# SP fetches each plain tile ahead of the shifted tile, and GpSimd fetches the coefficients of the last four blocks

## Chip, core and metric

One core of a Trainium2 chip runs the whole program. The metric is the device time of one launch in microseconds, the median of several runs. Its engines are PE (TensorE), DVE (VectorE), ACT (ScalarE), POOL (GpSimd) and SP (SyncE, which here only issues transfers). All transfers, whichever engine issues them, run on the core's 16 DMA engines.

## What is computed

```
x = x + _L0_conv_ref(_gn(x), L0_conv_offset)
x = x + _L1_conv_ref(_gn(x))
```

`x` is 16 images of 384 channels of 32 x 32 pixels, fp32. `_gn` is a group normalisation over 12 channels and all pixels of an image. `_L0_conv_ref` takes the 384 channels as 48 blocks of 8; each block is displaced by its own whole-pixel offset (zeros come in from outside) and then convolved with its own 3 x 3 Gaussian:

```
shifted = x[:, ch[:, None, None], iyc[:, :, None], ixc[:, None, :]]
shifted = shifted * mask[None]
out = lax.conv_general_dilated(shifted, kern_c[:, None, :, :], window_strides=(1, 1), padding='SAME', feature_group_count=C, ...)
```

Only blocks whose offset is under 32 pixels on both axes have anything left inside the image. `_L1_conv_ref` multiplies the 384 channels of every pixel by a Hadamard matrix.

## The kernel before

The program has four stages.

**Load and statistics** (to about 87 us): SP loads the 16 images into a ring of 12 places in SBUF, DVE and ACT take their statistics, and the coefficients of the group normalisation go to `gn_rows` in HBM (a semaphore `gn_out` marks them as written).

**The block stage** (about 88 to 133 us), which the change touches. `FAST` = 9 blocks (k = 0 to 8) are displaced and convolved. A tile holds one block as 128 partitions (16 images x 8 channels) of 1024 pixels, 512 KB. Each block needs two tiles from HBM and one small table:

- the *shifted* tile k (`fetch_shifted`, L302 to L306), read at the displaced address into one of `DEEP` = 3 buffers; it may be issued when PE has transposed shifted tile k-3 (`flipped`);
- the *plain* tile k (`fetch_plain`, L308 to L316), the same channels undisplaced, into one of `WIDE` = 5 buffers (`own_x`: three of `blk`, `other_a`, a piece of `parts`). Tiles 3 and 4 may be issued when block k-3 is finished by DVE (`x1_done`), because their buffers hold something else before that; tiles 5 to 8 when block k-5 has had its statistics and has *landed* in HBM (`blk_out`);
- the coefficients of block k (`fetch_gn`, L288 to L291): 128 x 2 numbers, 1 KB, from `gn_rows`.

Every fetch first reads its address from SBUF into a register (a TENSOR_LOAD) and then issues its transfer. SP fetches all of these but the coefficients of block 2, in an order written out by hand: shifted 0 to 4 and plain 0 to 2 already lie in SBUF or under way before the stage begins; then come the coefficients of 0, 1, 3, 4, and then for each k from 5 the coefficients of k, shifted k, plain k-2.

Per block, ACT subtracts the mean from the shifted tile (`centre`, L472), PE transposes it in 8 pieces (L578), ACT masks the upper and DVE the lower half of it (L491, L851), PE convolves by 20 matmuls (L588), DVE adds the result to the plain tile (`partial`, L855; for blocks 0 and 1 also L887) and takes its statistics (L874, L876), and POOL writes the finished tile to `x1_rows` in HBM (`leave`, L409; ACT writes its statistics, L484). PE's order is: transposes of k+1, then the convolution of k. DVE's is: mask of k+1, `partial` of k, statistics of k. The offset and convolution weights are ready long before.

POOL's only computing work in this stage is at its start: two products of 128 x 1024 (L415), for blocks 0 and 1, then the nine `leave`.

**Between the stages** (133 to 146 us): SP waits until all block statistics are in HBM, reads them back (L370), and the second normalisation's coefficients are worked out. POOL waits until all nine blocks have landed and then gathers them into the ring (L284).

**The Hadamard stage** (146 us to the end): 16 images are normalised, multiplied and stored; DVE is busy nearly throughout.

Of the kernel before, what the change touches and what calls it, by code (L numbers as in the profile page):

```python
# [33 lines left out]
DEEP = 3  # L34
WIDE = 5
EARLY = 2
FAST = 9
# [76 lines left out]
def build(nc, x_pad, offset, geo, had, out):  # L114
# [8 lines left out]
    with ctx:  # L123
# [3 lines left out]
        def sem(name):  # L127
            return ctx.enter_context(nc.semaphore(name))
# [103 lines left out]
        gn_out = sem("gn_out")  # L232
# [18 lines left out]
        def bc(ap, shape):  # L251
            return ap.broadcast_to(shape)
# [21 lines left out]
        def fast_blocks_out(eng):  # L274
            for u in range(WIDE):
                eng.wait_ge(blk_out[u], 16 * blocks_in(u))

        def gather_part(eng, n, limit, signal):

            first, count = PARTS[n]  # L280
            at = place_of(first + BATCH) if first < EXTRA else place_of(first)
            runs = x1_rows[0:limit, :].rearrange("c (g n) -> (c g) n", n=count * PIXELS)
            for t in range(CT):
                eng.indirect_dma_start(ring[:, t, at:at + count, :].rearrange("p b n -> p (b n)"), None,  # L284
                                       runs, bass.IndirectOffsetOnAxis(ap=row_at[:, n, t:t + 1], axis=0),
                                       bounds_check=limit * BATCH // count - 1, oob_is_err=False).then_inc(signal, 16)

        def fetch_gn(eng, k):  # L288

            at = eng.value_load(place[0:1, k, 0:1], min_val=0, max_val=CHANNELS - BIND)  # L290
            eng.dma_start(blk_gn[:, k, :], gn_rows[ds(at, BIND), :].rearrange("c (b k) -> b c k", k=2)).then_inc(gn_in[k], 16)  # L291
# [3 lines left out]
        def _(sp):  # L295
# [4 lines left out]
            def fetch_shifted(k):  # L300

                at = sp.value_load(place[0:1, k, 2:3], min_val=1, max_val=PIXELS * (CHANNELS - BIND + 2) - 1)  # L302
                if k >= DEEP:
                    sp.wait_ge(flipped, k - DEEP + 1)
                sp.dma_start(blk[:, DEEP + k % DEEP, :],
                             x_pad[:, ds(at, BIND * PIXELS)].rearrange("b (c n) -> b c n", c=BIND)).then_inc(shift_in[k % DEEP], 16)  # L306

            def fetch_plain(k):  # L308
                at = sp.value_load(place[0:1, k, 1:2], min_val=PIXELS, max_val=PIXELS * (CHANNELS - BIND + 1))  # L309
                if k >= WIDE:  # L310
                    sp.wait_ge(blk_stat_done, k - WIDE + 1)
                    sp.wait_ge(blk_out[k % WIDE], 16 * (k // WIDE))
                elif k >= DEEP:
                    sp.wait_ge(x1_done, k - DEEP + 1)
                sp.dma_start(own_x[k % WIDE],
                             x_pad[:, ds(at, BIND * PIXELS)].rearrange("b (c n) -> b c n", c=BIND)).then_inc(x_in[k % WIDE], 16)  # L316
# [21 lines left out]
            for k in (0, 1, 3, 4):  # L338
                fetch_gn(sp, k)
            for k in range(DEEP + EARLY, FAST + 2):  # L340
                if k < FAST:
                    fetch_gn(sp, k)
                    fetch_shifted(k)
                fetch_plain(k - 2)


            active = sp.value_load(count_i[0:1, 0:1], min_val=0, max_val=OFFSETS)
# [56 lines left out]
        @block.gpsimd  # L404
        def _(pool):
            def leave(k, u):

                pool.wait_ge(x1_done, k + 1)
                pool.dma_start(x1_rows[BIND * k:BIND * (k + 1), :].rearrange("c (b n) -> b c n", b=BATCH), own_x[u]).then_inc(blk_out[u], 16)  # L409


            image = [128, HEIGHT, WIDTH]
            for k in range(EARLY):
                pool.wait_ge(slope_ready, k + 1)
                pool.tensor_tensor(aside[k].rearrange("p (y x) -> p y x", y=HEIGHT),  # L415
                                   bc(share[:, k, 1, :].rearrange("p (y o) -> p y o", o=1), image),
                                   bc(share[:, k, 0, :].rearrange("p (o x) -> p o x", o=1), image), ALU.mult).then_inc(mean_share, 1)
            pool.wait_ge(rank_done, 1)
            pool.wait_ge(place_done, 1)
            for k in range(FAST):  # L420
                leave(k, k % WIDE)
            active = pool.value_load(count_i[0:1, 0:1], min_val=0, max_val=OFFSETS)

            fast_blocks_out(pool)
            with pool.If(active > FAST):
                pool.wait_ge(more_out, 32 * (OFFSETS - FAST))
            pool.wait_ge(rows_ready, 1)
            with pool.If(active > FAST):
                for n in range(KEPT):
                    gather_part(pool, n, CHANNELS, more_patched)  # L430
                pool.wait_ge(more_patched, 16 * CT * KEPT)
            for n in range(KEPT):
                gather_part(pool, n, FAST * BIND, part_in[n])
            for j in range(EXTRA):
                pool.wait_ge(reload_done[j], 16)
                with pool.If(active > FAST):
                    gather_part(pool, KEPT + j, CHANNELS, more_patched)
                    pool.wait_ge(more_patched, 16 * CT * (KEPT + j + 1))
                gather_part(pool, KEPT + j, FAST * BIND, part_in[KEPT + j])
# [544 lines left out]
```

## Time and profile before

| | |
|---|---|
| median of 3 runs | 258.5 us (257.35 to 259.47) |
| the profiled execution | 258.53 us, of it 256.7 us span |
| granted TensorE clock, mean | 0.862 |
| PE, DVE, ACT, POOL busy | 55%, 77%, 53%, 16% of the span |
| DMA | 76.79 MB, mean 299 GB/s |

In a row of the timeline the start and the duration stand first, then engine, line, operation, output<-inputs, count, and in brackets how long the engine sat idle before it and what released it. "SPq" is SP's sequencer. A TensorE clock of 1.00 is the upper of two levels and 0.50 the lower. In a table of stretches "DMA share" is the busy share of the 16 DMA engines; overlapping packets can put it a little over 1.

### The profile page before, as it was taken

How to read it: one execution, taken by the hardware profiler on the slowest of the kernel's cores; microseconds unless marked ns; L12 is line 12 of the kernel's file. 1: busy time of each engine (PE TensorE's matmuls, PEld its weight loads, DVE VectorE, ACT ScalarE, POOL GpSimd, SP SyncE). 2: the span in 40 equal slices, each digit the busy share in tenths (PEclk: the TensorE clock that was granted, in tenths of full speed). 3: DMA queues.
4: the chain of work that ended last, by engine and by line, in shares of the span. 5: the costliest groups of instructions: out<-in, count | busy, mean ns of one | idle time of the engine just before them, and what ended most of it. 6: DMA issues, size and time to landing. Idle time of an engine off the chain costs nothing.

```text
span 256.7 us, 2310 instructions
## 1 busy us (share of the span) xinstructions
PE 141.8 (55%) x616; PEld 85.4 (33%) x616; DVE 197.4 (77%) x321; ACT 136.2 (53%) x217; POOL 41.4 (16%) x39
## 2 busy tenths in 40 slices
PE   0000000607406349877921696999999999989610
PEld 0000000407406339776811522343333333333200
DVE  0799999999973179855750338999999999999930
ACT  1000999779762045143301399997787777770000
POOL 0000000000000052100113782000704383000000
PEclk9999999965955559979975569999999999999975
DMA  5999999999999307999970657229999999998798
GB/s 167 419 409 410 408 410 290 373 410 409 409 295 248 84 5 211 314 335 270 261 168 14 179 187 258 92 89 372 354 321 416 360 417 409 421 417 325 278 407 343
DMA packets 26222, 76.79 MB, mean 299 GB/s; under 512 B 7968, under 2 KB 8224, under 8 KB 25920
## 3 DMA queue, kind: packets, MB, share of 16 engines
q1 hardware_dynamic: 19616, 67.12, 72.0%
q0 software_dynamic: 4752, 9.45, 12.1%
q10 hardware_dynamic: 1840, 0.06, 0.5%
q8 instruction: 5, 0.08, 0.1%
q14 instruction: 9, 0.07, 0.1%
HBM read 67.07 MB, written 29.99 MB: 378 GB/s over the span
## 4 chain that ended last, share of the span: by engine, by line
DVE 39%; DMA 32%; SPq 10%; issue 6%; ACT 5%; PE 4%; ACTq 1%; DVEq 0%
DMA ring<-x_pad 27%; DVE ring L950 22%; DVE parts L272 10%; DMA blk<-x_pad 4%; ACT blk L533 3%; PE ps L569 2%; DVE blk L272 2%; SPq L291 2%; SPq L290 2%; ACT parts L541 2%; SPq L302 1%; PE ps L588 1%; DVE blk_half L874 1%; SPq L309 1%; DVE halfstat L814 1%
## 5 line engine op out<-in xcount | busy, mean ns | idle before, releaser
L950 DVE SCALAR_TENSOR_TENSOR ring<-ps,beta,ring 128x1024 f32<-128x1024 f32 x48 | 59.7, 1276 | 0.0
L650 PE MATMUL ps<-parts,had_sb 128*128 128x512 f16 x216 | 54.1, 385 | 8.0 <-DVE parts L272 5.7
L578 PE MATMUL ps<-geo_sb,blk 128*128 128x128 f32 x72 | 13.6, 353 | 57.5 <-DMA blk<-x_pad 45.2
L284 POOL DMA_INDIRECT ring<-x_rows,row_at x24 | 32.4, 1349 | 50.1 <-DMA ring<-x_pad 37.7
L814 DVE BATCH_NORM_STATS2 halfstat<-ring 128x6 f32<-128x512 f32 x64 | 38.8, 671 | 1.7 <-DMA ring<-x_pad 1.7
L533 ACT ACTIVATE blk<-ring,gn 128x1024 f32<-128x1024 f32 x32 | 37.8, 1225 | 0.0
L272 DVE TENSOR_TENSOR parts<-blk,parts 128x1024 f16<-128x1024 f32 x27 | 32.8, 1216 | 6.0 <-ACT parts L541 4.1
L588 PE MATMUL ps<-parts 128*128 128x160 f32 (+2 forms) x180 | 30.3, 329 | 10.6 <-ACT parts L463 10.2
L650 PEld LDWEIGHTS ps<-parts,had_sb 128*128 128x128 f16 x216 | 20.1, 99 | 44.0 <-DVE parts L272 13.2
L588 PEld LDWEIGHTS ps<-parts 128*128 128x128 f32 x180 | 29.0, 210 | 11.9 <-ACT parts L463 10.6
L660 PE MATMUL ps<-ring,first_w 128*128 128x512 f32 x64 | 32.0, 624 | 0.0
L578 PEld LDWEIGHTS ps<-geo_sb,blk 128*128 128x128 f32 x72 | 11.1, 182 | 58.8 <-issue 52.7
L541 ACT ACTIVATE parts<-blk 128x1024 f16<-128x1024 f32 x27 | 27.2, 1041 | 0.1
L472 ACT ACTIVATE blk<-blk,blk_gn 128x1024 f32<-128x1024 f32 x7 | 8.0, 1148 | 22.8 <-DMA blk<-x_pad 13.1
L453 ACT ACTIVATE other_a<-ring 128x1024 f32<-128x1024 f32 x16 | 18.3, 1143 | 0.0
L455 ACT ACTIVATE parts<-ring 128x1024 f32<-128x1024 f32 x16 | 18.3, 1141 | 0.0
L415 POOL TENSOR_TENSOR other_a<-parts 128x1024 f32<-128x1024 f32 x1 | 1.9, 1903 | 91.6 <-DVE parts L880 91.6
L660 PEld LDWEIGHTS ps<-ring,first_w 128*128 128x128 f32 x64 | 12.2, 198 | 10.7 <-issue 10.2
L525 ACT ACTIVATE first_w<-geo_sb,gn 128x128 f32<-128x128 f32 x16 | 6.4, 398 | 13.6 <-PE ps L650 12.4
L445 ACT ACTIVATE parts<-parts 128x396 f32<-128x396 f32 x1 | 0.5, 532 | 23.8 <-DVE parts L749 23.8
L569 PE MATMUL ps<-moment,geo_sb 128*128 128x16 f32 (+1 forms) x28 | 6.4, 389 | 11.6 <-DVE moment L835 11.6
L855 DVE SCALAR_TENSOR_TENSOR blk<-ps,blk_gn,blk 128x1024 f32<-128x1024 f32 x6 | 7.6, 1273 | 5.1 <-DMA blk<-x_pad 5.0
(115 smaller groups left out, 133.7 us busy)
## 6 DMA issues: line engine op xcount, KB each, us to landing
ring<-x_pad SPq DMA_DIRECT2D x20, 1536.0 KB, 15.3
out<-ring SPq DMA_DIRECT2D x13, 1536.0 KB
blk<-x_pad SPq DMA_DIRECT2D x15, 512.0 KB, 17.1
out<-ring SPq DMA_DIRECT2D x9, 512.0 KB
x_rows<-blk POOLq DMA_DIRECT2D x6, 512.0 KB, 7.5
other_a<-x_pad SPq DMA_DIRECT2D x2, 512.0 KB, 8.6
x_rows<-other_a POOLq DMA_DIRECT2D x2, 512.0 KB, 6.4
geo_sb<-geo SPq DMA_DIRECT2D x1, 683.0 KB, 4.6
```

The costliest lines, as they stand in the source:

```text
L272: eng.tensor_tensor(part_of(n, t, 1), scaled(n, t), part_of(n, t, 0), ALU.subtract).then_inc(low_done[t], 1)
L284: eng.indirect_dma_start(ring[:, t, at:at + count, :].rearrange("p b n -> p (b n)"), None, runs, bass.IndirectOffsetOnAxis(ap=row_at[:, n, ...
L453: act.activation(aside[0], image, ACT.Identity, bias=image[:, 0:1], scale=-1.0, accum_out=sums[:, 0, i:i + 1])
L455: act.activation(aside[1], image, ACT.Square, bias=image[:, 0:1], scale=-1.0, accum_out=sums[:, 1, i:i + 1]).then_inc(sum_stat_done, 1)
L533: act.activation(scaled(n, t), ring[:, t, place_of(i), :], ACT.Identity, bias=gn[:, t, i % BATCH, 1:2], scale=gn[:, t, i % BATCH, 0:1]).th ...
L541: act.activation(part_of(n, t, 0), scaled(n, t), ACT.Copy).then_inc(high_done[t], 1)
L578: last = pe.transpose(pixels[:, j // 4, 128 * (j % 4):128 * (j % 4 + 1)], shifted[:, 128 * j:128 * (j + 1)], eye)
L588: last = pe.matmul(sums[:, bank, 32 * (lo - 16 * bank):32 * (hi - 16 * bank)], pixels[:, j, :], weights[:, lo - (4 * j - 1):hi - (4 * j - ...
L650: last = pe.matmul(ps[n % 4][:, h, :], had_sb[:, sign, :], part_of(n, t, part)[:, 512 * h:512 * (h + 1)], start=False, stop=ends and part ...
L660: pe.matmul(ps[n % 4][:, h, :], first_w[:, n % 2, :], ring[:, 0, place_of(n + EXTRA), 512 * h:512 * (h + 1)], start=True, stop=False, skip ...
L814: last = dve.bn_stats(halfstat[:, i % 4, t, h, :], ring[:, t, place_of(i), 512 * h:512 * (h + 1)])
L950: dve.scalar_tensor_tensor(ring[:, m, place_of(i), :], ps[n % 4][:, :, :].rearrange("p a n -> p (a n)"), beta[:, i % BATCH:i % BATCH + 1], ...
```

## The change

SP's loop from k = 5 issues plain k-2 first and then shifted k, and no longer fetches coefficients. POOL fetches the coefficients of blocks 5 to 8 after its two products and before its first `leave`.

```
             for k in (0, 1, 3, 4):
                 fetch_gn(sp, k)
             for k in range(DEEP + EARLY, FAST + 2):
+                fetch_plain(k - 2)
                 if k < FAST:
-                    fetch_gn(sp, k)
                     fetch_shifted(k)
-                fetch_plain(k - 2)
...
+            pool.wait_ge(gn_out, 16)
+            for k in range(DEEP + EARLY, FAST):
+                fetch_gn(pool, k)
             pool.wait_ge(rank_done, 1)
             pool.wait_ge(place_done, 1)
             for k in range(FAST):
                 leave(k, k % WIDE)
```

Nothing else differs; the line numbers below the first hunk move by one or two.

On SP, at the start of the loop, the kernel before has the coefficients of block 5 (L290, L291), shifted 5 (L302, L305) and plain 3 (L309, L315, whose destination is `other_a`):

```order
L290 TENSOR_LOAD place
L290 ISA x2
L291 ISA
L291 DMA blk_gn<-gn_rows 128x1x2
L302 TENSOR_LOAD place
L302 ISA x2
L305 REGISTER_ALU [waits flipped]
L305 DMA blk<-x_pad 128x1x1024
L309 TENSOR_LOAD place
L309 ISA x2
L315 REGISTER_ALU [waits x1_done]
L315 DMA other_a<-x_pad 128x1x1024
```

The changed kernel has at the same place plain 3 and then shifted 5:

```order
L309 TENSOR_LOAD place
L309 ISA x2
L315 REGISTER_ALU [waits x1_done]
L315 DMA other_a<-x_pad 128x1x1024
L302 TENSOR_LOAD place
L302 ISA x2
L305 REGISTER_ALU [waits flipped]
L305 DMA blk<-x_pad 128x1x1024
```

The wait for `x1_done` now stands ahead of shifted 5. Near the loop's end, plain 5 (which waits for block 0 to have landed, `blk_out0`), shifted 7, plain 6 and shifted 8 stand in this order in the changed kernel:

```order
L315 REGISTER_ALU [waits blk_out0,blk_stat_done]
L315 DMA blk<-x_pad 128x1x1024
L302 TENSOR_LOAD place
L302 ISA x2
L305 REGISTER_ALU [waits flipped]
L305 DMA blk<-x_pad 128x1x1024
L309 TENSOR_LOAD place
L309 ISA x2
L315 REGISTER_ALU [waits blk_out1,blk_stat_done]
L315 DMA blk<-x_pad 128x1x1024
```

Before, each shifted tile stood ahead of that wait, so that shifted 7 and 8 waited for no block to land; now each stands behind one. On POOL the kernel before goes straight from the products to `leave`:

```order
L415 TENSOR_TENSOR other_a<-parts 128x1024 [waits slope_ready]
L415 TENSOR_TENSOR parts<-parts 128x1024 [waits slope_ready]
L409 DMA x_rows<-blk 16x8x1024 [waits x1_done,place_done,rank_done]
```

In the changed kernel the first of four coefficient fetches follows the products, and three more of the same four rows stand before the first `leave`:

```order
L414 TENSOR_TENSOR parts<-parts 128x1024 [waits slope_ready]
L290 TENSOR_LOAD place [waits gn_out]
L290 ISA x2
L291 ISA
L291 DMA blk_gn<-gn_rows 128x1x2
```

So four register loads and four issues have moved from SP, where they stood between tiles, to POOL, where they stand ahead of all nine writes of finished blocks.

## Rows read from the trace of the kernel before

**Rows 1.** The page's part 4: chain that ended last, by engine.

```profile
DVE 39%; DMA 32%; SPq 10%; issue 6%; ACT 5%; PE 4%; ACTq 1%; DVEq 0%
```

**Rows 2.** The chain in order of time: start us, us, what.

```profile
103.32 1.80 SPq L290
...
113.99 9.02 DMA blk<-x_pad
123.11 1.29 DVE blk L855
...
126.57 3.11 PE ps L588 x20
129.71 1.29 DVE other_a L855
```

**Rows 3.** Table of stretches: length, busy by engine (count), PEclk, DMA share, GB/s.

```profile
98.00:104.00 6.00, 6.00 (x47) 6.00 (x46) 5.86 (x10) 2.92 (x8) 1.66 (x3) 1.00 0.98 286
...
110.00:116.00 6.00, 5.37 (x28) 5.36 (x28) 3.34 (x5) 2.79 (x7) 0.52 (x1) 0.72 1.04 317
116.00:122.00 6.00, 4.16 (x30) 3.72 (x28) 3.34 (x5) 1.83 (x5) 0.52 (x1) 1.00 1.02 271
```

**Rows 4.** Timeline of SP: shifted 5, plain 3, shifted 7, plain 5, shifted 8, read-back.

```profile
96.58 0.56 SPq L305 DMA_DIRECT2D blk<-x_pad  x1
97.87 0.55 SPq L315 DMA_DIRECT2D other_a<-x_pad  x1
...
107.88 0.54 SPq L305 DMA_DIRECT2D blk<-x_pad  x1
110.06 0.54 SPq L315 DMA_DIRECT2D blk<-x_pad  x1
...
112.66 0.54 SPq L305 DMA_DIRECT2D blk<-x_pad  x1
...
137.49 0.38 SPq L370 DMA_DIRECT2D stat<-stat_rows  x1
```

**Rows 5.** Timeline of ACT and DVE: first uses of shifted 5 to 8, plain 5.

```profile
101.56 1.15 ACT L472 ACTIVATE blk<-blk,blk_gn 128x1024 f32<-128x1024 f32 x1 [2.81 <-issue]
...
114.81 1.15 ACT L472 ACTIVATE blk<-blk,blk_gn 128x1024 f32<-128x1024 f32 x1 [3.21 <-DMA blk<-x_pad]
...
117.26 1.28 DVE L855 SCALAR_TENSOR_TENSOR blk<-ps,blk_gn,blk 128x1024 f32<-128x1024 f32 x1 [2.60 <-DMA blk<-x_pad]
...
121.16 1.15 ACT L472 ACTIVATE blk<-blk,blk_gn 128x1024 f32<-128x1024 f32 x1 [4.17 <-DMA blk<-x_pad]
```

**Rows 6.** Timeline of PE: transposes and convolutions of blocks 5 to 8.

```profile
110.63 1.65 PE L578 MATMUL ps<-geo_sb,blk 128*128 128x128 f32 x8 [2.29 <-ACT blk L472]
112.08 4.16 PE L588 MATMUL ps<-parts 128*128 128x160 f32 x20
...
117.09 3.07 PE L588 MATMUL ps<-parts 128*128 128x160 f32 x20
122.36 1.09 PE L578 MATMUL ps<-geo_sb,blk 128*128 128x128 f32 x8 [2.20 <-ACT blk L472]
123.43 6.24 PE L588 MATMUL ps<-parts 128*128 128x160 f32 x40
```

**Rows 7.** Timeline of POOL at the start, and DVE's sums of blocks 0 and 1.

```profile
94.05 1.91 POOL L415 TENSOR_TENSOR parts<-parts 128x1024 f32<-128x1024 f32 x1
...
95.86 1.22 DVE L887 TENSOR_TENSOR blk<-blk,other_a 128x1024 f32<-128x1024 f32 x1
...
97.81 0.76 POOL L409 DMA_DIRECT2D x_rows<-blk  x1 [1.85 <-DVE blk L887]
...
99.12 1.22 DVE L887 TENSOR_TENSOR blk<-blk,parts 128x1024 f32<-128x1024 f32 x1
```

**Rows 8.** Views by line: L409's transfers, issue to landing; L422's register load.

```profile
DMA to landing us min/median/max: 5.5/7.5/10.2
...
L422 POOLq TENSOR_LOAD <-count_i x1: 497/497/497, 131.3 to 131.3; - x1
```

More of the change, by code:

```diff
@@ L340, in _ @@
             for k in range(DEEP + EARLY, FAST + 2):
+                fetch_plain(k - 2)
                 if k < FAST:
-                    fetch_gn(sp, k)
                     fetch_shifted(k)
-                fetch_plain(k - 2)
             active = sp.value_load(count_i[0:1, 0:1], min_val=0, max_val=OFFSETS)
@@ L417, in _ @@
                                    bc(share[:, k, 0, :].rearrange("p (o x) -> p o x", o=1), image), ALU.mult).then_inc(mean_share, 1)
+            pool.wait_ge(gn_out, 16)
+            for k in range(DEEP + EARLY, FAST):
+                fetch_gn(pool, k)
             pool.wait_ge(rank_done, 1)
```

## The prediction, written before the changed kernel was run

> **What bounds the kernel now.** I read the page's chain first. It runs mostly through DVE and DMA, but a tenth of it is SP's own queue [rows 1], which computes nothing. The chain in order of time shows where: from about 94 to 114 us it goes through SP alone, one register load and one issue after another, then through the landing of one tile (9.02 us, to 123.11), DVE, the last convolution (to 129.7) and the last `partial` [rows 2]. That landing is plain 6. One step of SP takes about 1.29 us (shifted 5 issued at 96.58, plain 3 at 97.87 [rows 4]), and more when the register load is slow (1.80 us once [rows 2]). In none of its steps from 96.58 to 117.92 does SP wait for a semaphore, so it looks like the bound of the stage.
>
> The table of stretches says something else. From 98 to 104 and from 110 to 122 us the DMA engines are full, a share of 0.98 to 1.04 [rows 3]. In this stage ten tiles are read and nine blocks are written. A transfer issued into full engines lands when those ahead of it are through, whatever its time of issue. So both readings have to be kept apart below: "issue counts" and "place in the queue counts".
>
> Then the landings. ACT and DVE sit idle until tiles land: shifted 5 is first used at 101.56 (the row names no tile, but the instruction waits only for the tile and its coefficients, so I take it as the landing), shifted 7 at 114.81, plain 5 at 117.26, shifted 8 at 121.16 [rows 5], plain 6 at 123.11 [rows 2]. From the first of these to the last are seven places in SP's queue (shifted 5, plain 3, shifted 6, plain 4, shifted 7, plain 5, shifted 8, plain 6), so one place is worth 21.55 / 7 = 3.08 us on average, the writes in between included, and 1.95 us between shifted 8 and plain 6.
>
> Last, what follows shifted 8. ACT centres it (1.15), PE transposes it (1.09, from 122.36) and then convolves blocks 7 and 8 (6.24, to 129.67) [rows 5, 6]; DVE adds block 8 at 129.71 [rows 2]. That is 8.55 us from landing to the last `partial`, with PE at work all the while once it has the tile. After plain 6 there is DVE's `partial` and statistics of block 6 and the mask of block 8, over at 126.5, just when PE comes to the convolution of 8 (126.57 [rows 2]). **So today both tiles end at the same time, and neither has slack.** The rest of the program hangs on block 8: its statistics are read back at 137.49 [rows 4], and a microsecond there is a microsecond at the end.
>
> **The change, part by part.**
>
> *The order of tiles at the start.* Plain 3 now stands ahead of shifted 5 and waits for block 0, whose sum ends at 95.86 + 1.22 = 97.08 [rows 7]. It goes out at about 97.15, where the first tile goes out at 96.58 today, and shifted 5 behind it at 98.45 (1.9 later). Plain 4 waits for block 1's sum, over at 99.12 + 1.22 = 100.34, so 100.4; shifted 6 follows at 101.7. The DMA engines start their ten tiles 0.57 us later: **+0.57**. Bounds: 0, if the later tiles catch up, and 0.6.
>
> *The four fetches on POOL.* POOL is free at 94.05 + 1.91 = 95.96 [rows 7]. The trace shows no coefficient fetch on POOL. From below it is SP's step, 1.0 to 1.29 us; from above, with POOL's one register load of 0.50 [rows 8] in place of SP's, 0.3 more. I take 1.29, since POOL's issue of a block (0.76 the first [rows 7]) is like SP's: four make 5.2 us, and the first `leave` goes out at 101.1, not at 97.81. What is queued behind: `leave` 0, 1 and 2, at about 101.1, 101.7 and 103.4, and plain 5 and 6 wait for the first two to land. Landing takes 5.5 to 10.2 us, median 7.5 [rows 8], so plain 5 goes out at about 108.6 (106.6 to 111.3), still 1.4 us ahead of today's 110.06 [rows 4]. Shifted 7 follows at 109.9, where today it goes out at 107.88; plain 6 at 111.2; shifted 8 at 112.5, as today (112.66). The fetches themselves land by about 104 and nobody waits for them.
>
> *Four fetches fewer on SP.* They save SP four steps of 1.3 to 2.3 us, but by the sum just made SP spends them on waiting for `leave` 0. Cover that hides it: none is needed, shifted 8 just doesn't go out sooner. **0**, and up to -2.1 if `leave` 0 and 1 land at their fastest (rival below). Of 1 KB each, the transfers cost the DMA engines nothing to speak of.
>
> The chain through SP speaks for more than 0 here, and the full DMA share for 0 [rows 2, 3]; I go by the share. The Trainium skill ("DMA: Bandwidth & Descriptors", section "Issuing engines are not separate DMA queues") says that issuing from more engines saves only the sequencer's issue time, usually small beside the transfer, since all transfers run on the same 16 engines. By that rule the sum would have 0 in this place, by the chain's rows up to -2.1. No run yet shows which.
>
> *The order of tiles at the end.* Shifted 8 moves from the seventh to the eighth place, plain 6 from the eighth to the seventh. If the place counts, shifted 8 lands where plain 6 does today. The bounds of one place are 1.95 (the distance at that very place) and 3.08 (the mean). I take 2.2, near the first: the distance at the place is the better witness, but with the writes of blocks coming later and blocks 4 and 5 perhaps sooner, one more piece of a write may fall in front. **+2.2.** Plain 6's earlier landing pays nothing back: DVE's `partial` of 6 needs convolution 6, for which PE first needs the transposes of block 7, and shifted 7 too has gone back one place (114.81 + 2.45, the distance to plain 5, is 117.3; centre, transposes and convolution make it 122.6, against 123.11 today).
>
> *Sum.* Shifted 8 lands at 121.16 + 0.57 + 2.2 = 123.9, the last `partial` starts 8.55 later at 132.5 and not at 129.71: +2.77. From the profiled execution's 258.53 this is 261.3; its time is that of the median (258.5), so nothing is corrected.
>
> **The rivals.**
>
> *Issue counts, not place (0.22).* Shifted 8 goes out at 112.5 as today, takes its 8.5 us as today, and lands at 121.0. Plain tiles come sooner, and the end stays bound by PE's 8.55 us behind shifted 8: 258.4 us. For it: SP never waits today, and the chain runs through it. Against: the DMA share.
>
> *Faster: the relief of SP reaches shifted 8 (0.13).* If `leave` 0 lands in 5.5 us (it goes out when the first four tiles are partly through), plain 5 goes out at 106.6, shifted 7 at 107.9, plain 6 at 109.2 and shifted 8 at 110.5, 2.15 before today. If a tile's landing keeps its 8.5 us, the last `partial` starts at 127.6, and shifted 7's own path (114.8 + 1.15 + 1.04 + 3.07 + 1.04 + 6.2) allows 127.3. That gives 256.4. It decides once `leave` 0 lands before about 107.5 and the DMA engines have idle time to give.
>
> *The clock falls as well (0.13).* PE waits for each shifted tile. In the stretch from 110 to 116 the granted clock is 0.72, and a convolution takes 4.16 us there where the next, at 1.00, takes 3.07 [rows 3, 6]; PE had stood idle for 2.29 us ahead of block 6's transposes just before [rows 6]. If shifted 7 and 8 come later, the idle stretches ahead of convolutions 7 and 8 grow, and at the lower level these two cost 1.1 us more each, 2.2 together: 263.5.
>
> *The forecast (0.52)* is 261.3, from 259.9 (one place at 1.95 and the start caught up, less 0.5 for a shorter gap before the last `leave`) to 262.7 (a place at 3.08 and 0.5 for sooner writes).
>
> **How the numbers follow.** About 1%, 2.6 us, is what a measurement of this kernel can tell from no change. The line to slower is 261.1, inside the forecast's own range: of its 0.52 I put 0.33 above and 0.19 within 1%. With the clock's 0.13 slower comes to 0.46; within 1% is 0.19 + 0.22, and I add 0.01 for the weaker half of the faster rival, 0.42; faster is 0.12. The range reaches down to 257.3, which leaves out most of the faster rival, and up to 264.0, the clock's rival with a little more.
>
> **What would show it.** In the profile after: plain 3 issued at 97.1 and shifted 5 at 98.5; the first `leave` at 101 rather than 97.8 (POOL's step); SP idle before plain 5 until `leave` 0 has landed, near 108.6; the first use of shifted 8 near 123.9 with ACT waiting for it, plain 6 landed some 2 us earlier with DVE not waiting for it; the last `partial` at 132.5; and the same distance from there to the end. If the share of DMA from 104 to 110 is well under 1, place in the queue didn't count there, and the sum is wrong towards less. If shifted 8 lands at 121 or before, the first or second rival holds. If convolution 7 or 8 takes over 4 us, the third does.

## The result: 0.8% slower, by 2.1 us

The changed kernel takes 260.74 us in the median of 13 runs, the kernel before, on the same chip, 258.06. The ratio is 1.0082, 95% interval 1.0057 to 1.0108: 1.5 to 2.8 us more. The ratio is taken from the fast runs alone; the two medians differ by 2.7 us. The forecast of 261.3 us, 2.77 more than before, is at the upper end of that. The change is under the 1% that the prediction took as the least difference to be told apart, but its interval excludes no change.

| | before | after |
|---|---|---|
| profiled execution, us | 258.53 | 261.39 |
| its span, us | 256.7 | 259.7 |
| first write of a block issued | 97.81 | 99.66 |
| shifted 5, 6, 7, 8 first used | 101.56, 109.43, 114.81, 121.16 | 105.25, 114.68, 119.00, 123.64 |
| last `partial` starts | 129.71 | 131.95 |
| block statistics read back | 137.49 | 139.03 |

The chain of the changed kernel over the whole run, by engine, on its page. SP's queue had 10% of it before [rows 1], PE 4%:

```profile
DVE 38%; DMA 31%; PE 12%; issue 7%; ACT 4%; SPq 2%; ACTq 1%; DVEq 0%
```

The same chain in order of time, from 100 us to the last block. This is the most telling view of the case:

```profile
100.46 0.54 SPq L315
...
101.04 1.56 SPq L302
...
103.03 11.62 DMA blk<-x_pad
114.65 0.02 issue
114.68 1.16 ACT blk L474
115.83 0.04 issue
115.88 1.97 PE ps L580 x8
117.85 3.75 PE ps L590 x20
121.60 0.87 PE ps L580 x8
122.47 2.83 PE ps L590 x20
125.31 0.87 PE ps L580 x8
126.18 5.74 PE ps L590 x40
131.92 0.02 issue
131.95 1.30 DVE other_a L857
```

Before, the chain ran through SP's issues to 113.99 and then through plain 6 [rows 2]. Now it leaves SP at 103.03, when *shifted 6* is issued, waits 11.62 us for that tile, and is then PE alone, without a gap, for 16 us. SP's timeline in the changed kernel:

```profile
97.22 0.57 SPq L315 DMA_DIRECT2D other_a<-x_pad  x1
98.52 0.54 SPq L305 DMA_DIRECT2D blk<-x_pad  x1
100.46 0.54 SPq L315 DMA_DIRECT2D parts<-x_pad  x1
103.03 0.54 SPq L305 DMA_DIRECT2D blk<-x_pad  x1
106.55 0.54 SPq L315 DMA_DIRECT2D blk<-x_pad  x1
108.47 0.54 SPq L305 DMA_DIRECT2D blk<-x_pad  x1
111.39 0.54 SPq L315 DMA_DIRECT2D blk<-x_pad  x1
112.67 0.54 SPq L305 DMA_DIRECT2D blk<-x_pad  x1
```

Plain 3 at 97.22, shifted 5 at 98.52 (before: 96.58 for shifted 5), plain 5 at 106.55 where it was 110.06, and shifted 8 at 112.67 where it was 112.66 [rows 4]. So SP's relief was spent, as forecast, before it reached shifted 8. It went into waits for finished blocks to land, of which SP had none before: between 94 and 120 us there are three of them in the changed kernel, 3.3 us together. ACT's first uses of the shifted tiles 5 to 8:

```profile
105.25 1.15 ACT L474 ACTIVATE blk<-blk,blk_gn 128x1024 f32<-128x1024 f32 x1 [6.55 <-issue]
...
114.68 1.15 ACT L474 ACTIVATE blk<-blk,blk_gn 128x1024 f32<-128x1024 f32 x1 [7.24 <-DMA blk<-x_pad]
...
119.00 1.15 ACT L474 ACTIVATE blk<-blk,blk_gn 128x1024 f32<-128x1024 f32 x1 [2.14 <-DMA blk<-x_pad]
...
123.64 1.15 ACT L474 ACTIVATE blk<-blk,blk_gn 128x1024 f32<-128x1024 f32 x1 [2.46 <-DMA blk<-x_pad]
```

All four are later than before [rows 5], shifted 5 by 3.7 us, 6 by 5.3, 7 by 4.2 and 8 by 2.5. And the table of stretches:

```profile
98.00:104.00 6.00, 6.00 (x43) 6.00 (x42) 5.86 (x10) 0.70 (x3) 2.56 (x5) 0.91 0.84 222
104.00:110.00 6.00, 4.45 (x31) 4.02 (x31) 4.37 (x8) 2.18 (x5) 0.52 (x1) 1.00 1.02 358
110.00:116.00 6.00, 0.73 (x6) 0.49 (x5) 2.78 (x4) 1.32 (x3) 0.52 (x1) 0.73 1.02 304
116.00:122.00 6.00, 6.00 (x34) 6.00 (x35) 1.06 (x2) 3.04 (x9) 0.00 (x0) 0.70 1.04 336
```

From 98 to 104 the DMA engines are at 0.84, where they were at 0.98 [rows 3]: the stage's transfers start later. From 104 on they are at 1.02 or more. PE is all but idle from 110 to 116 (0.73 us busy, before 5.37), and the granted clock is 0.70 in the stretch after it.

### The profile page after: what moved, and what is told of

Read it like the earlier page. It is cut to its first block, busy times and chain, and to the rows that moved or that the text cites. A ratio compares the mean times of both kernels' runs of the same rounds, so it can differ in the third digit from the quotient of the medians.

```text
span 259.7 us, 2312 instructions
## 1 busy us (share of the span) xinstructions
PE 143.9 (55%) x616; PEld 88.0 (34%) x616; DVE 197.8 (76%) x321; ACT 136.3 (52%) x217; POOL 40.4 (16%) x43
## 4 chain that ended last, share of the span: by engine, by line
DVE 38%; DMA 31%; PE 12%; issue 7%; ACT 4%; SPq 2%; ACTq 1%; DVEq 0%
DMA ring<-x_pad 27%; DVE ring L952 21%; DVE parts L272 10%; PE ps L590 5%; DMA blk<-x_pad 4%; PE ps L571 2%; PE ps L580 2%; PE ps L652 2%; ACT blk L535 2%; DVE blk L272 2%; ACT parts L543 1%; DVE blk_half L876 1%; DVE halfstat L816 1%; DVE blk L889 1%; PE ps L662 1%
## 5 line engine op out<-in xcount | busy, mean ns | idle before, releaser
L652 PE MATMUL ps<-parts,had_sb 128*128 128x512 f16 x216 | 55.1, 391 | 8.0 <-DVE parts L272 5.7
L284 POOL DMA_INDIRECT ring<-x_rows,row_at x24 | 29.3, 1223 | 54.0 <-DMA ring<-x_pad 41.8
L590 PE MATMUL ps<-parts 128*128 128x160 f32 (+2 forms) x180 | 31.4, 339 | 10.1 <-ACT parts L465 10.1
L590 PEld LDWEIGHTS ps<-parts 128*128 128x128 f32 x180 | 30.5, 218 | 10.7 <-ACT parts L465 10.5
L652 PE MATMUL ps<-blk,had_sb 128*128 128x512 f16 x40 | 10.3, 380 | 1.5 <-DVE blk L272 1.5
```

What stands on the lines that cost most here:

```text
L590: last = pe.matmul(sums[:, bank, 32 * (lo - 16 * bank):32 * (hi - 16 * bank)], pixels[:, j, :], weights[:, lo - (4 * j - 1):hi - (4 * j - ...
L652: last = pe.matmul(ps[n % 4][:, h, :], had_sb[:, sign, :], part_of(n, t, part)[:, 512 * h:512 * (h + 1)], start=False, stop=ends and part ...
```

## The experiments

Two theories. **Theory 1:** the cost is a tile's place in the queue of full DMA engines, so it comes from the order of the tiles and has little to do with who issues the coefficients. **Theory 2:** the coefficient fetches on POOL, which push back the first write of a block, and SP's waits behind it, make the cost. All ratios are against the kernel before on the same chip. Single executions of one kernel scatter by 1 to 1.5 us either way; a profile shows one of them, so sizes are taken from ratios and mechanisms from profiles. Each profile is one execution, and a mechanism read from it is shown for that execution.

### The order of tiles alone

```
             for k in range(DEEP + EARLY, FAST + 2):
+                fetch_plain(k - 2)
                 if k < FAST:
                     fetch_gn(sp, k)
                     fetch_shifted(k)
-                fetch_plain(k - 2)
```

> Only the order of tiles is changed (plain k-2, then the coefficients, then shifted k); all fetches stay on SP. Theory 1 (a tile's place in the full DMA queue counts, the order of tiles costs nearly all): 1.5 to 2.7 us slower than before, as the whole change is. Theory 2 (the coefficient fetches on POOL, which push back the first write, cost it): within 0.6 us of before.

Measured, over six runs: 1.0206 (1.0156 to 1.0256), 5.3 us slower. Theory 1 named the right part, but neither named the size: this half alone costs more than twice the whole change. ACT's first uses of the shifted tiles and, below, two issues of SP (shifted 5 and shifted 8), in its profile:

```profile
107.31 1.15 ACT L472 ACTIVATE blk<-blk,blk_gn 128x1024 f32<-128x1024 f32 x1 [8.78 <-DMA blk<-x_pad]
113.74 1.15 ACT L472 ACTIVATE blk<-blk,blk_gn 128x1024 f32<-128x1024 f32 x1 [4.26 <-DMA blk<-x_pad]
...
124.94 1.15 ACT L472 ACTIVATE blk<-blk,blk_gn 128x1024 f32<-128x1024 f32 x1 [4.84 <-DMA blk<-x_pad]
```

```profile
101.23 0.54 SPq L305 DMA_DIRECT2D blk<-x_pad  x1
...
116.07 0.55 SPq L305 DMA_DIRECT2D blk<-x_pad  x1
```

Shifted 5 goes out at 101.23, where the changed kernel has 98.52: behind the wait of plain 3 stand the coefficients of block 5 and slow register loads. Every tile after it goes out 2.1 to 4.5 us later than in the changed kernel, shifted 8 by 3.4. So here SP's issuing *does* count: the chain of this kernel runs through SP up to shifted 8's issue at 116.07, through its landing, and through PE to the end of the stage. SP waits for no block to land here. The share of the DMA engines doesn't give this away. From 110 to 122 it is full, as in the changed kernel, and only the rate in the last column is lower (271 and 244 GB/s, there 304 and 336):

```profile
110.00:116.00 6.00, 4.82 (x31) 4.39 (x30) 2.85 (x4) 2.17 (x5) 0.52 (x1) 0.89 1.04 271
116.00:122.00 6.00, 5.96 (x42) 5.54 (x42) 3.98 (x8) 2.17 (x5) 0.52 (x1) 1.00 1.01 244
```

### The fetches on POOL alone

Against the kernel before:

```
             for k in range(DEEP + EARLY, FAST + 2):
                 if k < FAST:
-                    fetch_gn(sp, k)
                     fetch_shifted(k)
                 fetch_plain(k - 2)
...
+            pool.wait_ge(gn_out, 16)
+            for k in range(DEEP + EARLY, FAST):
+                fetch_gn(pool, k)
```

> Only the fetches of coefficients 5 to 8 are moved to POOL; the order of tiles stays shifted k, plain k-2. Theory 1: the full DMA engines take back what SP saves, 0.5 us slower to 1.5 us faster than before. Theory 2: 1.5 us or more slower, by the first write going out some 2 us later and plain 5 with shifted 8 behind it.

Measured: 0.9992 (0.9967 to 1.0017), no change. Theory 2 falls for the fetches by themselves. What SP saved shows at its issues (shifted 8 here at 108.99, 3.7 us sooner than before), and where most of it went shows at the landings: shifted 8 is first used at 119.59, only 1.6 us sooner. The last `partial` starts at 129.45, 0.3 us sooner. The rest went to PE, which idled 4.93 us until shifted 7 came and then took 4.34 us for convolution 6 (granted clock 0.57 from 116 to 122). The median time from issue to landing of the seven tiles that SP fetches into `blk` between 94 and 122 us (last column, us), in the kernel before:

```profile
blk<-x_pad SPq DMA_DIRECT2D x7, 512.0 KB, 8.0
```

with the fetches on POOL alone:

```profile
blk<-x_pad SPq DMA_DIRECT2D x7, 512.0 KB, 9.8
```

with the order alone:

```profile
blk<-x_pad SPq DMA_DIRECT2D x7, 512.0 KB, 6.2
```

and with both, the changed kernel:

```profile
blk<-x_pad SPq DMA_DIRECT2D x7, 512.0 KB, 10.5
```

The first tile of the stage in the kernel before, issued at 96.58 into idle engines, landed in 4.9. A tile that goes out sooner into full engines waits longer. In the order alone tiles land in 6.2 us and SP's late issues set the pace. That fits with one and the same move being worth nothing in the kernel before (-0.08%) and 1.2% in the changed order (2.06% less 0.82%; by the two intervals 0.7 to 1.8%). The medians alone don't prove it: the kernel of the next section with only the last pair exchanged has 6.7, and it issues its tiles at nearly the times of the kernel before, which has 8.0.

### One pair at a time

Only plain 6 ahead of shifted 8, and in a second kernel (with `DEEP + EARLY + 1` in place of `FAST - 1`) only plain 4 ahead of shifted 6, all fetches on SP:

```
             for k in range(DEEP + EARLY, FAST + 2):
+                if k == FAST - 1:
+                    fetch_plain(k - 2)
                 if k < FAST:
                     fetch_gn(sp, k)
                     fetch_shifted(k)
-                fetch_plain(k - 2)
+                if k != FAST - 1:
+                    fetch_plain(k - 2)
```

> The kernel before with one exchange: plain 6 ahead of shifted 8. If the cost of the change lies where the prediction put it (shifted 8 one place later): 1.5 to 2.2 us slower than before, with shifted 8 first used near 123.2 and the last partial near 131.8. If it lies at shifted 6, as the trace after the change suggests (PE without a gap behind shifted 6, used at 114.68): under 1 us slower, and shifted 8's lateness alone reaches the end only in part.

> The kernel before with one exchange: plain 4 ahead of shifted 6. If shifted 6 is what the order of tiles makes late: shifted 6 first used 2 us or more after 109.4 and the kernel 1 us or more slower. If shifted 8 alone counts: within 0.6 us of before, since shifted 7 and 8 keep their places.

Measured: 1.0074 (1.0045 to 1.0104) for the last pair, 1.9 us, and 1.0042 (1.0013 to 1.0070) for the second, 1.1 us. The exchange at shifted 8 costs what the prediction said for one place (1.95 to 2.2), in the kernel that has nothing else changed; the interval is 1.2 to 2.7 us. The profiled execution of the last pair doesn't show it: at 257.36 us it was the fastest of its twelve, and shifted 8 is used at 121.18 in it, as before. The ratio stands, its mechanism is not shown by that trace. In the second pair's profile shifted 6 is used at 114.31, 4.9 us later than before, and PE idles behind it as in the changed kernel. So either pair costs by itself. The second pair's profiled execution is 2 us above the median of its runs, so its 4.9 us may be more than the usual.

### The start kept

Against the changed kernel:

```
-            for k in range(DEEP + EARLY, FAST + 2):
+            fetch_shifted(DEEP + EARLY)
+            fetch_plain(DEEP)
+            for k in range(DEEP + EARLY + 1, FAST + 2):
                 fetch_plain(k - 2)
                 if k < FAST:
                     fetch_shifted(k)
```

> The changed kernel, but shifted 5 is still issued ahead of plain 3; from plain 4 on the order is the changed one (plain 4, shifted 6, plain 5, ...). By the prediction's term for the start (+0.57): 0.6 us faster than the changed kernel, 1.5 us slower than before. If the start is what makes shifted 6 late (place and first wait together): within 0.6 us of before.

Measured: 1.0044 (1.0013 to 1.0074). Against the changed kernel's 1.0082 the start is worth 0.38%, 1.0 us, more than the 0.57 of the prediction; the intervals of the two overlap, so the size is uncertain. The other 0.44%, 1.1 us, is what the order from plain 4 on costs with the fetches on POOL. In this kernel's profile shifted 6 is used at 109.97, as early as before, though it goes out at 103.10, when the changed kernel's does (103.03). Here shifted 8 sets the end as the prediction had it: used at 122.13, with PE idle for 1.27 us ahead of its transposes, and the last `partial` 8.22 us later, at 130.35.

### Shifted tiles further ahead

Against the changed kernel:

```
             for k in range(DEEP + EARLY, FAST + 2):
-                fetch_plain(k - 2)
                 if k < FAST:
                     fetch_shifted(k)
+                if k > DEEP + EARLY:
+                    fetch_plain(k - 3)
+            fetch_plain(FAST - 1)
```

> POOL fetches the coefficients; SP issues shifted tiles one place further ahead than before (shifted 5, shifted 6, plain 3, shifted 7, plain 4, shifted 8, plain 5, then plain 6 to 8). If both kinds of tile are needed at the same time in the order of before (neither has slack), shifted 8 gains a place and more and plain 6 keeps its own: within 0.6 us of before, with DVE waiting for plain tiles. If shifted tiles alone count: 1.5 us or more faster than before.

Measured: 1.0022 (0.9982 to 1.0063). Shifted 8 is used at 116.30 in its profile, 4.9 us sooner than before, and nothing is gained: plain 4 is added at 114.23 where it was 111.25 before. In this profile, then, moving one kind of tile ahead took from the other, which fits the prediction's reading that neither has slack in the order of before.

### Less to transfer: half writes

```
-                pool.dma_start(x1_rows[BIND * k:BIND * (k + 1), :].rearrange("c (b n) -> b c n", b=BATCH), own_x[u])
+                pool.dma_start(x1_rows[BIND * k:BIND * (k + 1), :].rearrange("c (b n) -> b c n", b=BATCH)[:, :, 0:PIXELS // 2], own_x[u][:, 0:PIXELS // 2])
...
             fetch_gn(act, EARLY)
+            act.dma_start(x1_rows[0:FAST * BIND, :].rearrange("c (b n) -> c b n", b=BATCH)[:, :, PIXELS // 2:],
+                          ring[0:FAST * BIND, 0, 0:8, :].rearrange("c a (h n) -> c (a h) n", h=2))
```

> The kernel before, but each finished block writes only half of its pixels to HBM (the other half is filled from unrelated data in one write ahead of the stage, so the result is not the reference's). Full DMA engines bound the stage: tiles land sooner though they are issued at the same times, shifted 8 about 4 us sooner (near 117), and the kernel is 2.5 to 4.5 us faster. SP's issuing bounds it: within 1 us of before.

> The changed kernel with the same halved writes. If the change costs through a tile's place in a full queue, the places cost less once the queue is short: the distance between this and the other halved kernel is under 1 us where the distance between the full ones is 2.1. If it costs through SP's waits for blocks (sums and landings), the distance stays at 2 us.

Measured: 1.0054 (1.0017 to 1.0090) on the kernel before and 1.0202 (1.0133 to 1.0271) on the changed one. Both expectations of theory 1 missed, and the profile says why the pair can't be read as meant: the filling write was issued at 90 us, just ahead of the stage, and the first coefficients, which land in 2 us otherwise, took 7.6 to 9.6 behind it. The stage began 7.6 us late (`partial` of block 2 at 109.46, before 101.82) and then ran 6.5 us faster to the last `partial` (21.4 us against 27.9). But shifted 5 went out only 2.5 us late (99.09), so SP was that much further ahead of the stage, and either bound would have shortened it. The experiment had a fault, and it decides nothing.

### Less to transfer: half reads

The ten tiles of the stage are read for 512 of 1024 pixels; nothing is added ahead.

```
-                sp.dma_start(blk[:, DEEP + k % DEEP, :],
-                             x_pad[:, ds(at, BIND * PIXELS)].rearrange("b (c n) -> b c n", c=BIND))
+                n = PIXELS // 2 if k >= DEEP + EARLY else PIXELS
+                sp.dma_start(blk[:, DEEP + k % DEEP, 0:n],
+                             x_pad[:, ds(at, BIND * PIXELS)].rearrange("b (c n) -> b c n", c=BIND)[:, :, 0:n])
```

and plain tiles from 3 on alike.

> The kernel before, but the ten tiles that SP fetches during the stage (shifted 5 to 8, plain 3 to 8) are read for half of their pixels only; the rest of a tile keeps older data. The stage's start is left alone, which the halved writes did not do. Full DMA engines bound the stage: 5 to 7 us faster, the last partial near 124, about 3.7 us a block. Issuing on SP bounds it (all ten go out at the same times): at most 3 us faster, since shifted 8 still goes out at 112.7 and needs some 5 us to land.

> The changed kernel with the same halved reads. If the order costs through places in a full queue: within 0.7 us of the other halved kernel. If it costs through SP's waits for the sums of blocks 0 and 1 and for blocks 0 to 3 to land: still 2 us or more slower than the other halved kernel.

Measured: 0.9893 (0.9855 to 0.9932) on the kernel before, 0.9848 (0.9793 to 0.9902, four runs) on the changed one. **The cost of the change is gone**: with short queues it is 1.2 us *faster* than the other, within both intervals, so no difference is shown, but 2.1 us slower is excluded. The seven tiles now land in 5.2 us before the change:

```profile
blk<-x_pad SPq DMA_DIRECT2D x7, 256.0 KB, 5.2
```

and in 5.4 after it:

```profile
blk<-x_pad SPq DMA_DIRECT2D x7, 256.0 KB, 5.4
```

That is theory 1's expectation for the pair, but the pair doesn't single out the places in the queue. SP waits for no block to land in the halved changed kernel, since the writes land sooner too, so its waits are gone with the queue. And both halved kernels have SP on the chain up to shifted 7 or 8, so the fetches on POOL can have paid back a cost of the order, as they did in full queues (1.2%). The size for the kernel before missed: 2.8 us faster and not 5 to 7. With the queue short, SP's issuing comes forward as the bound (shifted 8 goes out at 111.46 there and lands 5.3 us later), and the clock fell after a gap on PE. These two PE rows are the transposes of block 7 after a gap, and convolution 6 behind them (3.0 us at the upper level). Not every gap did this: in the order alone PE idled 2.87 us ahead of block 8's transposes, and the clock stayed at 1.00.

```profile
113.95 1.09 PE L580 MATMUL ps<-geo_sb,blk 128*128 128x128 f32 x8 [2.03 <-ACT blk L474]
115.03 4.74 PE L590 MATMUL ps<-parts 128*128 128x160 f32 x20
```

### Addresses in registers

All addresses are read into registers while SP waits for the normalisation's coefficients, so that SP has no register load in the stage. The edit is shown for the order of before; in the changed order POOL still loads and fetches for blocks 5 to 8.

```
+            for k in (0, 1, 3, 4, 5, 6, 7, 8):
+                load_gn(sp, k)
+            for k in range(DEEP + EARLY, FAST):
+                ready["shifted", k] = sp.value_load(place[0:1, k, 2:3], ...)
+            for k in range(DEEP, FAST):
+                ready["plain", k] = sp.value_load(place[0:1, k, 1:2], ...)
             sp.wait_ge(gn_done, 1)
```

> The kernel before, in its own order, with all addresses of the stage read into SP's (and for block 2 ACT's) registers ahead of it, so that a step of SP is 0.65 us and never has a slow register load. At the stage's start the first coefficients go out some 0.5 us sooner and all five by 2.5 us sooner: about 0.7 us faster for that by itself. If the full DMA engines bound the rest, 0.5 to 1.5 us faster in all, like the kernel with the fetches on POOL plus this start; if issuing bounds it, 3 us or more.

> The changed kernel with the same addresses in registers. If the changed order costs by issuing (SP behind its first wait and slow loads): the cost of the order goes, within 0.7 us of the other kernel with registers. If it costs by places and by the waits for blocks themselves: still 1.5 us or more slower than the other.

Measured: 0.9981 (0.9949 to 1.0014) in the order of before, 1.0089 (1.0056 to 1.0122) in the changed one. With SP's issuing made cheap in both, the change still costs 1.1%, 2.8 us (by the two intervals 1.6 to 4.0). So it costs by places in the queue and by the waits for blocks, not by the price of SP's steps. Both show in the profiles. In the order of before shifted 8 goes out at 105.42 and is used at 117.87; in the changed one it goes out 2.7 us later, right behind plain 6, for which SP waited until block 1 had landed (its write went out at 99.81, plain 6 at 107.40), and is used 4.1 us later. How the 2.8 us divide between place and wait isn't shown. Shifted 8 in the order of before:

```profile
105.42 0.54 SPq L312 DMA_DIRECT2D blk<-x_pad  x1
```

SP's issues of plain 5, shifted 7, plain 6 and shifted 8 in the changed order with registers:

```profile
104.71 0.54 SPq L326 DMA_DIRECT2D blk<-x_pad  x1
105.43 1.12 SPq L314 DMA_DIRECT2D blk<-x_pad  x1
107.40 0.54 SPq L326 DMA_DIRECT2D blk<-x_pad  x1
108.11 0.54 SPq L314 DMA_DIRECT2D blk<-x_pad  x1
```

Shifted 8, the last of these, is issued at 108.11, 4.6 us sooner than in the changed kernel, and first used at 121.98, 13.9 us later. The seven tiles take, in that kernel:

```profile
blk<-x_pad SPq DMA_DIRECT2D x7, 512.0 KB, 11.8
```

This is the full queue at its plainest. Registers by themselves gave 0.2%, 0.5 us, with an interval that includes no change: no complete version here is clear of noise faster than the kernel before.

## Why the prediction was right, and where it was not

- **What bounds the stage before: right, and borne out.** Moving shifted 8's issue 3.7 us forward (fetches on POOL) gives nothing in the time, and making every step of SP cheap gives 0.2%, within the noise. Of the 3.7 us the landing took back 2.1. What the prediction took as its witness, the full DMA share, is a weak one: the order alone has it too, and is bound by issuing.
- **The start, +0.57: right in place, too small.** Plain 3 went out at 97.22 (97.15 forecast), shifted 5 at 98.52 (98.45). Keeping the start gave back 1.0 us; the whole queue starts later (DMA at 0.84 from 98 to 104), and shifted 6, used at 114.68, came at 109.97 with the start kept.
- **The fetches on POOL: right in sum, wrong in detail.** The first write went out at 99.66, not 101.1. POOL's first register load ran beside its product, so the first fetch began at 95.90. Plain 5 therefore went out at 106.55, not 108.6, and shifted 8 at 112.67 (112.5 forecast). The section on the change is wrong in one point: before it, shifted 8 too stood behind a wait for a block, that of plain 5 for block 0, and only shifted 7 did not. In the trace of before this wait cost nothing; the change put shifted 8 behind block 1's as well. The Trainium skill ("DMA: Bandwidth & Descriptors", section "Issuing engines are not separate DMA queues") says that issuing from another engine saves issue time only. In the order of before that was worth nothing here (ratio 0.9992), as the rule has it; in the changed order SP's time was what ran short, and it was worth 1.2%. The prediction had no such case: it took SP's relief as 0 whatever the order, and by its terms the order alone would have cost 2.8 us and not 5.3. That 5.3 less 3.2 comes out near its 2.77 is partly luck.
- **The place of shifted 8, +2.2: right in size, and not the only path to the end.** The exchange by itself cost 1.9 us, though its own profile doesn't show how. In the changed kernel shifted 8 was first used at 123.64 (123.9 forecast), and the last `partial` started 8.31 us later (8.55 forecast), so the step "shifted 8 lands, and 8.55 us later the last `partial` starts" came within 0.3 us. What the prediction missed is a second path of the same length. The chain goes back to shifted 6, used at 114.68, two tiles earlier than the prediction looked, and the last `partial` is 17.3 us away from there. PE was still at work on what shifted 6 had left it when block 8's tile was ready (124.8), and began on it at 125.14. The two paths end within 0.3 us of each other: with shifted 8 alone, at the 8.22 us of the kernel with the start kept, the last `partial` would have started at 131.9 by this estimate, and it started at 131.95. The prediction followed shifted 7's path and found it harmless, and never made that sum for 6, which had gone back a place behind a later start.
- **The clock, the third rival: it came, elsewhere.** PE stood idle for 5.27 us before block 6's transposes, and the clock went to the lower level for them and for convolution 5. These two PE rows are the transposes and the convolution:

```profile
115.88 1.97 PE L580 MATMUL ps<-geo_sb,blk 128*128 128x128 f32 x8 [5.27 <-ACT blk L474]
117.64 3.96 PE L590 MATMUL ps<-parts 128*128 128x160 f32 x20
```

  Against 1.04 and 3.00 that is some 1.9 us on the chain. Hardly any of it reached the end: block 8's tile was ready only 0.3 us before PE came to it. And the kernel before had much the same at the same place (1.65 and 4.16 [rows 6]), off its chain. Convolutions 7 and 8 kept the upper level.
- **The sum.** The last `partial` moved by 2.24 us (2.77 forecast) in the profiled execution, whose span grew by 3.0. At the first weights of the Hadamard stage (145.67 before, 148.25 after) the distance is 2.6; the remaining 0.4 us arise inside that stage and were not traced further. This execution is 0.65 us above its kernel's median. The exchange at shifted 8 (1.9) and the start (1.0), measured one by one, add up to more than the 2.1 of the whole.
- **"Issue counts, not place"** falls for the kernel before (fetches on POOL: no change) and for the change (shifted 8 issued at the same time, used 2.5 us later). **"Faster"** falls: plain 5 did go out at 106.6, that rival's figure, but plain 6 waited again and went out at 111.39 and not 109.2, so that shifted 8 went out at 112.67 and not 110.5. Nor did a tile's landing keep its 8.5 us: shifted 8 was used 11.0 us after its issue.

What stays open: how the cost of the order divides between places in the queue and waits for blocks, why landings differ so between profiles that issue at nearly the same times (shifted 6, issued at 103.03 and 103.10, took 11.6 us in the changed kernel and 6.8 with the start kept), why some register loads take 1 to 2 us in this stage, and the last 0.4 us.

## What to carry to other kernels

Before giving a queue's issuer less to do, compare the time from issue to landing with that of a lone transfer: where it is much longer, as here (8.0 to 10.5 us against 4.9), a transfer issued sooner mostly waits longer, and the order of the queue is what there is to choose. A full busy share of the DMA engines doesn't tell this by itself. Measure the parts of a change alone and together: what one part is worth can depend on the other. When two kinds of tile share a queue, work out for *each* tile, not only the last, when its consumer is free; a tile late in the middle sets the end if the engine behind it then runs without a gap. A wait that is put ahead of a fetch on an in-order queue can cost every fetch behind it.

## What the runs showed of the hardware that was not expected

- Two halves of a change that do not add: +2.06% and -0.08% alone, +0.82% together.
- POOL's sequencer took a register load ahead while the engine still worked: its second product ran from 94.05 to 95.96, the load of the first coefficient fetch began at 94.0, and the fetch went out at 95.90, so the first write went out 3.8 us later, at 99.66, and not 5.2 us later.
- Transfers of 1 KB on SP's queue, issued behind one of 2.25 MB on ACT's, took 7.6 to 9.6 us to land, where the first of them, issued before it, took 2.0: a queue of one's own was no protection.
- The busy share of the DMA engines was 1.01 to 1.04 both where issuing set the pace (244 to 271 GB/s) and where it didn't (304 to 336 GB/s).
